# A selective scan laid out as 4 states by 32 channels instead of 1 state by 128 channels

## The reference, cut to what matters

```python
x = x + 0.5 * ffn(layernorm(x))
x = x + small_scan(layernorm(x))
x = x + 0.5 * ffn(layernorm(x))
x = x + 0.5 * experts(layernorm(x))
x = x + large_scan(layernorm(x))      # this part changes
x = x + 0.5 * experts(layernorm(x))

def large_scan(x):                    # 256 channels, 16 states, chunks of 32 positions
    xc, res = split(x @ W_in.T + b_in)
    u = silu(causal_conv(xc))                          # (512, 256)
    dlt, B, C = split(u @ W_x.T)                       # 64, 16 and 16 wide
    delta = softplus(dlt @ W_dt.T + b_dt)              # (512, 256)
    A = -exp(A_log)                                    # (256, 16)
    # for every channel d and state n, along t, restarted every 32 positions:
    #   h[t] = exp(delta[t, d] * A[d, n]) * h[t-1] + delta[t, d] * B[t, n] * u[t, d]
    #   y[t, d] = sum over n of h[t, d, n] * C[t, n]
    return (y * silu(res)) @ W_out.T + b_out
```

## Time and profile before

| | us |
|---|---|
| median of 3 runs | 1054.3 |
| lowest, highest | 1046.0, 1056.8 |
| the profiled execution, its own time | 1056.0 |
| its span, first to last instruction | 1054.3 |
| outside its span | 1.7 |

### The profile page before, as it was taken

How to read it: one execution, slowest core, us unless ns; L and a number is a source line. 1 busy time by engine, 2 the same in 40 slices (tenths; PEclk the granted TensorE clock), 3 DMA queues, 4 the chain that set the end, 5 groups by cost and what they waited for, 6 DMA issues and landing times.

```text
span 1054.3 us, 11228 instructions
## 1 busy us (share of the span) xinstructions
PE 911.8 (86%) x3358; PEld 431.3 (41%) x3358; DVE 768.3 (73%) x1717; ACT 655.8 (62%) x1030; POOL 516.0 (49%) x412
## 2 busy tenths in 40 slices
PE   6557877888889888999999999999999889978975
PEld 5334334343444344445354444435443343333432
DVE  3222514988599769995999688978998989799821
ACT  4435558568757866677778765897687437634221
POOL 2112135555647464645565555666475545555311
PEclk9668898999899989999999999999999898998976
DMA  3000106523553446336337545545354717665320
GB/s 144 10 0 25 67 0 217 196 100 124 197 190 111 137 175 227 116 130 213 136 122 233 186 154 171 190 168 198 128 185 171 236 47 254 222 190 184 107 90 11
DMA packets 49325, 151.83 MB, mean 144 GB/s; under 512 B 4976, under 2 KB 13296, under 8 KB 49264
## 3 DMA queue, kind: packets, MB, share of 16 engines
q1 hardware_dynamic: 49264, 151.12, 41.9%
HBM read 148.21 MB, written 2.88 MB: 143 GB/s over the span
## 4 chain that ended last, share of the span: by engine, by line
PE 47%; DVE 26%; ACT 12%; issue 6%; POOL 5%; DMA 2%; SPq 0%; DVEq 0%; POOLq 0%; ACTq 0%
PE yp L1484 10%; DVE dA L983 10%; PE mp L1428 4%; PE mp L1443 4%; PE fp L1249 4%; PE pp L1363 4%; PE pp L1229 3%; PE fp L1265 3%; ACT L117 3%; DVE hs L990 3%; DVE he L941 2%; PE mp L1229 2%; PE pp L1333 2%; ACT dA L1208 2%; PE mp L1452 2%
## 5 line engine op out<-in xcount | busy, mean ns | idle before, releaser
L710 POOL TENSOR_TENSOR dbu<-du,b_row 128x1024 f32<-128x1024 f32 x128 | 301.5, 2359 | 169.7 <-DVE dA L983 151.0
L983 DVE TENSOR_TENSOR_SCAN dA<-dA,dbu 128x512 f32<-128x512 f32 x256 | 312.4, 1220 | 67.5 <-POOL dbu L710 34.9
L1484 PE MATMUL yp<-hs,ident 128*128 128x512 f32 x512 | 268.4, 628 | 14.1 <-DVE hs L990 13.9
L1208 ACT ACTIVATE dA<-delta,pr 128x512 f32<-128x512 f32 x256 | 173.6, 685 | 80.5 <-DVE hs L990 76.3
L990 DVE TENSOR_TENSOR hs<-dA,c_row 128x512 f32<-128x512 f32 x256 | 176.9, 691 | 9.8 <-PE yp L1484 1.1
L117 ACT ACT_TABLE_LOAD x130 | 166.8, 1283 | 2.4
L1484 PEld LDWEIGHTS yp<-hs,ident 128*128 128x128 f32 x512 | 89.2, 195 | 142.6 <-issue 84.8
L1428 PE MATMUL mp<-cont,ex_ 64*128 64x512 f32 x128 | 79.1, 701 | 12.7 <-DVE he L941 11.4
L1265 PE MATMUL fp<-w,hT 128*128 128x129 f32 x512 | 68.6, 285 | 13.7 <-ACT hT L1044 7.0
L1432 PE MATMUL mp<-cont,ex_ 64*128 64x512 f32 x128 | 79.3, 703 | 0.1
L1265 PEld LDWEIGHTS fp<-w,hT 128*128 128x128 f32 x512 | 64.2, 197 | 36.4 <-ACT hT L1044 14.9
(11 more groups left out here) (216 smaller groups left out, 1353.8 us busy)
## 6 DMA issues: line engine op xcount, KB each, us to landing
b_row<-held SPq DMA_DIRECT2D x104, 512.0 KB, 4.9
c_row<-held SPq DMA_DIRECT2D x104, 512.0 KB, 4.3
gsp<-gheld SPq DMA_DIRECT2D x64, 512.0 KB, 6.2
xin<-L_attn_x SPq DMA_DIRECT2D x8, 256.0 KB, 4.7
out<-xb SPq DMA_DIRECT2D x8, 256.0 KB, 3.4
ex_<-c_ex SPq DMA_DIRECT2D x1, 1001.0 KB, 6.8
b_row<-c_ps SPq DMA_DIRECT2D x1, 768.0 KB, 8.2
pr<-c_pr SPq DMA_DIRECT2D x1, 567.0 KB, 9.1
```

The lines of the kernel that those rows point to most:

```text
L710: pool.tensor_tensor(out=dbu[:, j % 2, :].rearrange("p (r t) -> p r t", r=2), in0=d, in1=b_n, op=ALU.mult).then_inc(dbu_r.sem, 1)
L983: dve.tensor_tensor_scan(out=dA[:, half], data0=dA[:, half], data1=dbu[:, j % 2, half], initial=0.0, op0=ALU.mult, op1=ALU.add).then_inc(h ...
L1208: act.activation(out=dA[:, r * SEQ:(r + 1) * SEQ], in_=delta[:, i % 2, c, :], func=ACT.Exp, scale=mA[:, c, 2 * k + r:2 * k + r + 1]).then_ ...
L1484: pe.matmul(yp[:, :], lhsT=ident[:, :], rhs=hs[:, j % 2, r * SEQ:(r + 1) * SEQ], start=(s % PAIRS == 0 and r == 0), stop=(s % PAIRS == PAI ...
```

## The change

The partitions are dealt out anew in the scan: 4 blocks of 32 partitions. Block s holds states 4s to 4s+3 (`OWN` = 4), each partition of a block a channel (a lane). The 256 channels are 8 groups of 32 lanes (`GROUPS`), 4 groups per chunk (`PER`). A step takes one of a block's four states and two channel groups, one in each half; so one instruction works on 4 states by 32 channels in each half. There are again 16 steps to a batch.

- u*delta and delta must stand in all four blocks. Each chunk of each goes from `du` and `delta` to DRAM (`uheld`, `dheld`, 256 KB) and comes back in four transfers of 256 KB, one for each block, into `u4` and `d4`. These have one buffer each, as `du` and `delta` now have; SP waits, for each chunk, until the batch before has used it.
- B and C of a batch come to `bc4` in two halves (states 0 and 1, states 2 and 3 of the blocks), four transfers of 256 KB each; `W_x` is reordered on the host so that the rows lie right. One buffer; each half waits until the batch before is through with it.
- A is stored a second time in the new layout (a column of `mA` for each group and own state); the smallest allowed decay is applied to eight slices of it instead of two.
- GpSimd makes delta*u and the restarts a chunk at a time. Once, at the start, it makes `stack`, 128x32: four 32x32 identities on top of each other.
- TensorE adds the four states and puts the result into the group's own 32 partitions of `yp`, with `stack` as the stationary tile; it waits for both halves of a step and then issues both matmuls.
- VectorE's product with C waits, on the first half, for both sums of the step before last.
- The lists `ORDER` of all engines are new (SP has a further thread, U, for u and delta); they are left out here.

```diff
-PAIRS = STATES // 2
-STEPS = IC * PAIRS
-B_SLOTS, C_SLOTS = 3, 3
-
-
-STEP_ORDER = [(0, k) for k in range(PAIRS)] + [(1, k) for k in reversed(range(PAIRS))]
...
+BLOCKS = 4
+OWN = STATES // BLOCKS
+LANES = P // BLOCKS
+GROUPS = INNER // LANES
+PER = GROUPS // IC
+STEPS = IC * OWN * PER // 2
+C_STEPS = STEPS // IC
+
+
+STEP_ORDER = [(c, k, j) for c in range(IC) for k in range(OWN) for j in range(PER // 2)]
+
+
+def block_rows(s):
+    return slice(LANES * s, LANES * (s + 1))
+
+
+def last_of_half(h):
+    return max(s for s, (c, k, j) in enumerate(STEP_ORDER) if k // 2 == h) + 1
...
-        b_row = sb("b_row", [P, B_SLOTS, 2 * SEQ])
-        c_row = sb("c_row", [P, C_SLOTS, 2 * SEQ])
+        d4 = sb("d4", [P, GROUPS, SEQ])
+        u4 = sb("u4", [P, GROUPS, SEQ])
+        bc4 = sb("bc4", [P, 2, 2, 2, SEQ])
+        stack = sb("stack", [P, LANES])
...
-        delta = sb("delta", [P, 2, IC, SEQ])
-        du = sb("du", [P, 2, IC, SEQ])
+        delta = sb("delta", [P, IC, SEQ])
+        du = sb("du", [P, IC, SEQ])
...
-            def spread():
+            def rows():
                 for i in range(BATCH):
                     yield True
                     sp.wait_ge(bc_r.sem, bc_r.at(i, 1))
                     if i >= 2:
-                        for rows, arrived in ((B_ROWS, b_in), (C_ROWS, c_in)):
-                            for at in range(rows.slots):
-                                sp.wait_ge(arrived[at], 16 * rows.loads_before(at, (i - 1) * STEPS))
-                    sp.dma_start(held[i % 2, :, :, :].rearrange("s n t -> (s n) t"), dbc[64:96, :]
+                        for h in range(2):
+                            sp.wait_ge(bc_in[h].sem, bc_in[h].at(i - 2, 16 * BLOCKS))
+                    sp.dma_start(held[i % 2, :, :, :].rearrange("h s (w t) -> (h s w) t", t=SEQ), dbc[64:96, :]
                                  ).then_inc(bc_out.sem, 16)
-                    for s, (c, k) in enumerate(STEP_ORDER):
...
+                    for h in range(2):
+                        yield True
+                        if h == 0:
+                            sp.wait_ge(bc_out.sem, bc_out.at(i, 16))
+                        if i >= 1:
+                            sp.wait_ge(dbu_r.sem, dbu_r.at(i - 1, last_of_half(h)))
+                            sp.wait_ge(hc_r.sem, hc_r.at(i - 1, 2 * last_of_half(h)))
+                        for s in range(BLOCKS):
+                            sp.dma_start(bc4[block_rows(s), h, :, :, :].rearrange("p w k t -> p (w k t)"),
+                                         held[i % 2, h, s:s + 1, :].broadcast_to([LANES, 4 * SEQ])
+                                         ).then_inc(bc_in[h].sem, 16)
+
+            def deltas():
+                for i in range(BATCH):
+                    for c in range(IC):
+                        by_lane = lambda a: a[i % 2, c, :, :].rearrange("(g r) t -> r g t", r=LANES)
+                        own = slice(c * PER, (c + 1) * PER)
+                        yield True
+                        sp.wait_ge(du_r.sem, du_r.at(i, c + 1))
+                        if i >= 2:
+                            sp.wait_ge(u_in[c].sem, u_in[c].at(i - 2, 16 * BLOCKS))
+                        sp.dma_start(uheld[i % 2, c, :, :], du[:, c, :]).then_inc(u_out[c].sem, 16)
+                        yield True
+                        sp.wait_ge(start_r.sem, start_r.at(i, c + 1))
+                        if i >= 2:
+                            sp.wait_ge(d_in[c].sem, d_in[c].at(i - 2, 16 * BLOCKS))
+                        sp.dma_start(dheld[i % 2, c, :, :], delta[:, c, :]).then_inc(d_out[c].sem, 16)
+                        yield True
+                        sp.wait_ge(u_out[c].sem, u_out[c].at(i, 16))
+                        if i >= 1:
+                            sp.wait_ge(dbu_r.sem, dbu_r.at(i - 1, (c + 1) * C_STEPS))
+                        for s in range(BLOCKS):
+                            sp.dma_start(u4[block_rows(s), own, :], by_lane(uheld)).then_inc(u_in[c].sem, 16)
+                        yield True
+                        sp.wait_ge(d_out[c].sem, d_out[c].at(i, 16))
+                        if i >= 1:
+                            sp.wait_ge(dA_r.sem, dA_r.at(i - 1, 2 * (c + 1) * C_STEPS))
+                        for s in range(BLOCKS):
+                            sp.dma_start(d4[block_rows(s), own, :], by_lane(dheld)).then_inc(d_in[c].sem, 16)
...
-                pool.wait_ge(del_r.sem, del_r.at(i, IC))
-                pool.wait_ge(mx_ps.sem, mx_ps.at(i, 1))
-                pool.tensor_tensor(out=du[:, b, :, :], in0=delta[:, b, :, :], in1=du[:, b, :, :],
-                                   op=ALU.mult).then_inc(du_r.sem, 1)
-                pool.wait_ge(du_r.sem, du_r.at(i, 1))
-                starts = delta[:, b, :, :].rearrange("p c (k t) -> p c k t", t=CHUNK)[:, :, :, 0]
-                pool.tensor_copy(out=starts, in_=m_far[:, :, :]).then_inc(start_r.sem, 1)
+                for c in range(IC):
+                    yield True
+                    pool.wait_ge(del_r.sem, del_r.at(i, c + 1))
+                    pool.wait_ge(mx_ps.sem, mx_ps.at(i, 1))
+                    pool.tensor_tensor(out=du[:, c, :], in0=delta[:, c, :], in1=du[:, c, :],
+                                       op=ALU.mult).then_inc(du_r.sem, 1)
+                    pool.wait_ge(du_r.sem, du_r.at(i, c + 1))
+                    starts = delta[:, c, :].rearrange("p (k t) -> p k t", t=CHUNK)[:, :, 0]
+                    pool.tensor_copy(out=starts, in_=m_far[:, c, :]).then_inc(start_r.sem, 1)
...
+                step(pool.memset(stack[:, :], 0.0))
+                for s in range(BLOCKS):
+                    ins = pool.affine_select(out=stack[:, :], in_=stack[:, :], compare_op=ALU.not_equal, fill=1.0,
+                                             base=-LANES * s, pattern=[[-1, LANES]], channel_multiplier=1)
+                    if s < BLOCKS - 1:
+                        step(ins)
+                ins.then_inc(consts, 1)
...
-                    for s, (c, k) in enumerate(STEP_ORDER):
-                        j = i * STEPS + s
-                        yield True
-                        if s == 0:
-                            pool.wait_ge(du_r.sem, du_r.at(i, 1))
-                        pool.wait_ge(b_in[B_ROWS.slot[j]], 16 * B_ROWS.load[j])
-                        if j >= 2:
-                            pool.wait_ge(hs_r.sem, 2 * (j - 1))
-                        d = du[:, i % 2, c, :].rearrange("p (a t) -> p a t", a=1).broadcast_to([P, 2, SEQ])
-                        b_n = b_row[:, B_ROWS.slot[j], :].rearrange("p (r t) -> p r t", r=2)
-                        pool.tensor_tensor(out=dbu[:, j % 2, :].rearrange("p (r t) -> p r t", r=2),
-                                           in0=d, in1=b_n, op=ALU.mult).then_inc(dbu_r.sem, 1)
+                    for s, (c, k, j) in enumerate(STEP_ORDER):
+                        n = i * STEPS + s
+                        yield True
+                        if s % C_STEPS == 0:
+                            pool.wait_ge(u_in[c].sem, u_in[c].at(i, 16 * BLOCKS))
+                        pool.wait_ge(bc_in[k // 2].sem, bc_in[k // 2].at(i, 16 * BLOCKS))
+                        if n >= 2:
+                            pool.wait_ge(hs_r.sem, 2 * (n - 1))
+                        b_n = bc4[:, k // 2, 0, k % 2, :].rearrange("p (a t) -> p a t", a=1)
+                        pool.tensor_tensor(out=dbu[:, n % 2, :].rearrange("p (r t) -> p r t", r=2),
+                                           in0=u4[:, c * PER + 2 * j:c * PER + 2 * j + 2, :],
+                                           in1=b_n.broadcast_to([P, 2, SEQ]), op=ALU.mult).then_inc(dbu_r.sem, 1)
...
-                        for c in range(IC):
-                            ch.add(dve.tensor_scalar(out=mA[:, c, :], in0=mA[:, c, :], scalar1=m_low[:, c:c + 1],
-                                                     scalar2=-1.0, op0=ALU.max, op1=ALU.mult))
+                        for g in range(IC, IC + GROUPS):
+                            ch.add(dve.tensor_scalar(out=mA[:, g, 0:OWN], in0=mA[:, g, 0:OWN],
+                                                     scalar1=m_low[:, g:g + 1], scalar2=-1.0, op0=ALU.max,
+                                                     op1=ALU.mult))
...
                             dve.wait_ge(dA_r.sem, h + 1)
                             if r == 0:
-                                dve.wait_ge(dbu_r.sem, j + 1)
-                            dve.tensor_tensor_scan(out=dA[:, half], data0=dA[:, half], data1=dbu[:, j % 2, half],
+                                dve.wait_ge(dbu_r.sem, n + 1)
+                            dve.tensor_tensor_scan(out=dA[:, half], data0=dA[:, half], data1=dbu[:, n % 2, half],
                                                    initial=0.0, op0=ALU.mult, op1=ALU.add).then_inc(hs_r.sem, 1)
                             dve.wait_ge(hs_r.sem, h + 1)
                             if r == 0:
```

(41 more changed lines are left out.)

164 lines of the change are left out of this document (70 added, 94 removed).

## The result

The changed kernel takes 1106.6 us (median of 4 runs, 1100.3 to 1111.0), the kernel before 1053.2 in the same session: ratio 1.051, interval 1.043 to 1.059. It is slower by 5%; 1002 was forecast. The profiled execution took 1104.7 us, 1102.9 of them span, at a mean granted clock of 0.87 (0.94 before).

The account below looks back on a forecast made before the run. TensorE (92% busy in the middle), then VectorE, was taken as the bound. Lead 181, middle 756 (VectorE's 703.0 at 93%), tail 63.3 and 1.7 around the span gave 1002 us, 5% faster; range 970 to 1042.

Parts of the forecast that it names:

- the sums: TensorE's adds into yp: a step takes 1.0 us in place of 2.10, so TensorE loses 141 us.
- the first scan: Batch 0: VectorE's new list puts a copy ahead of the scan, which starts at 181 instead of 173.
- 141 table loads: ScalarE loads 141 tables instead of 130, 14 us more, hidden by its slack.
- the boundary's idle time: Between two batches' scans: VectorE's 43.7 idle us go, since the next scan's inputs lie ready.
- the step that decided: Batch boundary: u and delta round trips are hidden behind the scan before, priced at nothing; uncovered, 10 to 16 us each.
- the same term from the transfers' side: Round trips of u and delta through DRAM: about 10 us each, 16 if queued, hidden and priced at nothing.
- the share: Middle, first scan to last gating product: VectorE busy 93% instead of 86%, so 703.0 us of work take 756.
- the second sum: Cross-check from VectorE's waits at boundary, gating product and exponentials: 62 us less at most, 994, agreeing with 1002.
- (b): Column groups don't overlap for the half sums; TensorE keeps 751.6 us, only boundaries gain: 1020; chance 0.10.
- (c): TensorE's granted clock takes the gain: mean falls to 0.85, total 1045, no measurable change; chance 0.12.
- (d): The scan starves on its transfers at batch boundaries: slower, 1100 to 1164 at worst; chance 0.08.
- a sign of being wrong: In the scan: VectorE waiting for yp as before, exponentials waiting for d4, or middle's mean clock under 0.9.

Follow-up runs that it names:

- before_halfyp: The kernel before, with every second sum matmul into yp cut from 512 columns to 32: 1058.5 us, ratio 1.005 to the kernel before.
- after_nooverlap: The changed kernel with a step's two sums made one after the other through a zero-padded 128x64 stationary tile: 1123.6 us, ratio 1.066 to the kernel before.

## Why the prediction was wrong, point by point

*Right:* the sums (138.5 us busy for about 130, a step of four records in 1.05 us for 1.0), the first scan (182 for 181), 141 table loads, the tail, and the boundary's idle time, which went (one stretch without a scan is still 8.7 us, over the 8 named). Timeline of TensorE in the changed kernel, one step's sums between its neighbours, and the group of all sums:

```profile
634.23 1.12 PE L1358 MATMUL pp<-m_zT,ro 128*128 128x512 f32 x2
635.28 1.05 PE L1511 MATMUL yp<-hs,stack 128*32 128x512 f32 x4
636.27 1.98 PE L1254 MATMUL pp<-s,ro 128*128 128x512 f32 x4
```

```profile
L1511 PE MATMUL yp<-hs,stack 128*32 128x512 f32 x512 | 138.5, 678 | 35.7 <-DVE hs L1011 35.6
```

The drain that the Trainium skill's "TensorEngine Tiling (Array Packing)", "Key Properties", speaks of shows no price here either: the sums start 1.05 us behind the pair ahead of them, and what follows starts 0.99 us behind them.

*Wrong, the step that decided:* "So it is hidden ... and the 43.7 idle us go as well ... I price this at nothing". I asked only when du would be ready, not what the work that makes it would push aside. To have d4 and u4 there in time, the new order moves the next batch's front (silu, softplus, the gelus beside them, the gates) to the middle of the scan, and ScalarE and SyncE hand out decays and gates in that same order. Shown: the boundary's idle time did go, by 37 us, and 75 us came up inside the scans; the waits for decays come with this order whatever is scanned (57.7 us here, 54.1 without trips, 60.9 with the old tiles).

*Wrong, the same term from the transfers' side:* the trips cost 27 us of the middle (861.0 with them, 833.9 without), some 30 of the time, where nothing was put down. Gates and rows queue behind them, and 32 partitions take them in at 207 GB/s. I had given 10 us for a trip and nothing for who stands behind it.

*Wrong, the share:* "I take 93%" came from windows clear of the boundary, beside a full TensorE; over the eight whole stretches it was 91% before. It was to be 756 us of middle with 53 idle; it was 861 with 152.7 idle, a share of 82%, and without trips still 85%, the 86% of before. That TensorE's fill held VectorE back was never shown by those rows, and before_halfyp says that in the old order its relief, with the clock that it brought, gave nothing: 52 us off TensorE in the scan, and not one came out. In the new order the relief does count (16 us by the version without overlap).

*Wrong, the second sum:* "The same from the waits" adds 43.7 us of boundary and half of the 32.9 at the gating product. Of these 32.9 us, 28.9 lie in the very stretches between the scans, as this line of the first one shows (263.5 to 274.8, before):

```profile
DVE yg L998 <- PE yp L1484: 10.2, 1, 10.2
```

So it counted the same time twice, and that the two sums agreed was no check. It also says how little VectorE waited for yp inside the scans.

*The rivals:* (b) is out. (c): the mean clock in the middle was 0.89, under the 0.9 that I had named, and TensorE's other matmuls took 718.0 us for 643.4, over half of what the sums had freed. With the clock back at 0.92 (after_nooverlap) the kernel was slower, but there the sums took 98.7 us more, so the runs don't separate the clock from the relief. The Trainium skill's "TensorE: Matmul & The Clock Gate", section "Why this matters for your kernels", asks for no idle gaps between bursts of matmuls; the trace agrees in that the clock of the middle fell from 0.97 to 0.89 as TensorE's busy share fell from 92% to 80%. But (c) gave 1045, and the time came out 60 us worse. (d) had the sign and the range (1100 to 1164), for the most part not the place. ScalarE and GpSimd did wait for d4 and u4, which I had named as a sign of being wrong:

```profile
ACT dA L1233 <- DMA d<-dheld: 13.4, 4, 4.2
```

```profile
POOL dbu L729 <- DMA u<-uheld: 21.6, 2, 12.4
```

But 4.2 and 9.2 us of that stand ahead of the first scan, and the 12.4 at one boundary, that of batch 6. Most of what VectorE lost it lost behind what was pushed aside: 45.6 of its 57.7 us for decays fall in the first three batches, where neither engine waited for d4 or u4 behind the first scan.

*Open:* why the layout gives VectorE nothing in either order. Without trips its middle is 16 us over before's; in the old order VectorE waits for sums 53.2 us (34.0 before) although they take half of TensorE's time. That TensorE's other matmuls at a lower clock (0.90) stand ahead of them in its order would fit, but was only argued.

## What to carry to other kernels

Idle time between two stages is no gain until you have said what its late work displaces when it is moved up: count what else the same engine and the same queue hand out from that spot. Before a change relieves an engine because it is 92% busy, run the old kernel with half of that work left out; it is one run, and here it gave 1.005. Before you add up waits and idle stretches, see that they don't lie in the same time. Price a transfer by its form as well as by its bytes, and name the transfers that queue behind it.

## What the runs showed of the hardware

A transfer into 32 partitions kept all 16 transfer engines busy and moved 207 GB/s, the same bytes over 128 partitions 321. One whose memory side was four blocks of 32 rows, against 128 rows of the tile, used a quarter of the engines (share 0.25, 95 GB/s) and the changed kernel took 1334.9 us with it, 21% more; the Trainium skill's "DMA: Bandwidth & Descriptors", section "Why a DMA increments its semaphore by 16 and not by 1", ties the number of engines to the slowest dimension of both sides, and four of 16 agrees. A sum cut from 512 columns to 32 still took 265 ns a record, where the full one took 678.
